# Half a first chain, loads on SyncE's queue, and softmax denominators summed on VectorE

## What is computed

```python
w_down = down_project * dg[b] + db[b];  w_up = up_project * ug[b] + ub[b]   # per batch, from cond_512
h = relu(x @ w_down) @ w_up + x                                             # low-rank adapter
paths = sigmoid(h @ Wp + bp)                                                # 8 heads, 5 levels
agree = pq * pk + (1 - pq) * (1 - pk);  sim = cumprod(agree).sum() / 5      # every query with every key
attn = softmax(where(causal, sim, -inf));  x = x + (attn @ (h @ Wv)) @ Wo
z = x @ (U[b] @ V) + bias;  U = (mu @ W_dec + b_dec)                        # batch's own weights
out = z + z @ expert_w[argmax(z @ gate_w.T)]                                # one of 8 experts
```

## Time and profile before

| | |
|---|---|
| median of 3 runs | 154.97 us |
| the profiled execution, its time | 155.55 us |
| its span, first to last instruction | 153.4 us |
| busy: TensorE, VectorE, ScalarE, GpSimd | 141.2 (92%), 83.7 (55%), 58.8 (38%), 31.2 (20%) us |
| chain that ended last: TensorE, VectorE, ScalarE | 83%, 11%, 2% |
| granted TensorE clock, mean | 0.998 |

### The profile page before, as it was taken

How to read it: one execution, slowest core, us unless ns; L and a number is a source line. 1 busy time by engine, 2 the same in 40 slices (tenths; PEclk the granted TensorE clock), 3 DMA queues, 4 the chain that set the end, 5 groups by cost and what they waited for, 6 DMA issues and landing times.

```text
span 153.4 us, 5078 instructions
## 1 busy us (share of the span) xinstructions
PE 141.2 (92%) x2296; PEld 89.8 (59%) x2296; DVE 83.7 (55%) x156; ACT 58.8 (38%) x70; POOL 31.2 (20%) x56
## 2 busy tenths in 40 slices
PE   5989678999497999999999999999999999999992
PEld 5746155554274777457656655567558577666650
DVE  0563532619966378296915483558146851985431
ACT  3013156264226342558333451573434447310010
POOL 7200004100405302640022205200222440110000
PEclk9999999999999999999999999999999999999999
DMA  4989999600011200000101000100011010110112
GB/s 121 311 320 433 448 376 353 209 4 0 0 22 17 35 0 4 0 4 0 37 3 38 34 4 0 38 0 4 34 38 38 0 38 0 38 38 34 68 38 71
DMA packets 7381, 12.50 MB, mean 81 GB/s; under 512 B 1552, under 2 KB 5808, under 8 KB 7232
## 3 DMA queue, kind: packets, MB, share of 16 engines
q10 hardware_dynamic: 2496, 7.23, 12.1%
q1 hardware_dynamic: 4768, 4.89, 9.9%
q0 software_dynamic: 96, 0.05, 1.1%
HBM read 9.95 MB, written 2.22 MB: 79 GB/s over the span
## 4 chain that ended last, share of the span: by engine, by line
PE 83%; DVE 11%; ACT 2%; issue 1%; POOL 0%; ACTq 0%; POOLq 0%; DVEq 0%
PE work L561 36%; PE c_ps L561 24%; PE s_ps L561 17%; PE work L738 3%; DVE rden L420 2%; DVE feat L552 2%; PE work L678 2%; DVE tiles L509 1%; ACT prob L365 1%; DVE h_t L455 1%; ACT phi_t L390 1%; DVE u_row L481 1%; PE work L730 1%; DVE x_t L541 1%; DVE logit L464 0%
## 5 line engine op out<-in xcount | busy, mean ns | idle before, releaser
L365 ACT ACTIVATE prob<-s_ps 128x1536 f32<-128x1536 f32 (+1 forms) x24 | 38.2, 1593 | 39.3 <-PE s_ps L561 36.3
L420 DVE RECIPROCAL rden<-c_ps 128x256 f32<-128x256 f32 x16 | 28.1, 1757 | 26.5 <-PE c_ps L561 26.5
L342 POOL TENSOR_SCALAR_AFFINE_SELECT prob<-prob 128x1024 f32<-128x1024 f32 x16 | 20.1, 1257 | 93.1 <-ACT prob L365 93.1
L561 PE MATMUL s_ps<-phi_t 32*128 32x256 f32 (+1 forms) x384 | 24.2, 365 | 1.6 <-ACT phi_t L390 1.0
L561 PE MATMUL c_ps<-prob,v_sb 128*32 128x256 f32 (+1 forms) x384 | 24.9, 346 | 0.0
L561 PEld LDWEIGHTS s_ps<-phi_t 32*128 32x128 f32 x384 | 17.4, 184 | 10.6 <-issue 6.8
L561 PE MATMUL work<-ctx_t,mix_sb 128*32 128x256 f32 x256 | 17.0, 381 | 0.4
L561 PE MATMUL work<-zo_t,gexp 128*32 128x256 f32 x256 | 16.9, 379 | 0.0
L561 PEld LDWEIGHTS c_ps<-prob,v_sb 128*32 128x32 f32 x384 | 11.5, 109 | 9.0 <-issue 2.0
L561 PE MATMUL c_ps<-prob,ones 128*32 128x256 f32 (+1 forms) x256 | 16.3, 326 | 0.0
L561 PE MATMUL work<-w_vl,h_t 128*32 128x296 f32 x208 | 14.8, 416 | 1.1 <-DVE h_t L455 0.6
(11 more groups left out here) (95 smaller groups left out, 133.4 us busy)
## 6 DMA issues: line engine op xcount, KB each, us to landing
wdec<-in_W_dec ACTq DMA_DIRECT2D x1, 3855.0 KB, 15.2
x_t<-in_x_tr SPq DMA_DIRECT2D x4, 512.0 KB, 9.3
ex_t<-in_expert_tr ACTq DMA_DIRECT2D x1, 2048.0 KB, 22.1
...
```

What stands on the lines that cost most here:

```text
L342: nc.gpsimd.affine_select(out=tri, in_=tri, compare_op=ALU.is_ge, fill=0.0, base=0, pattern=[[0, HG], [0, 2], [1, P]], channel_multiplier= ...
L365: nc.scalar.activation(prob[:, p % 2, :, 0:width(p)], s_ps[:, :, 0:width(p)], ACT.Exp).then_inc(exped, 1)
L420: link(nc.vector.reciprocal(rden[:], c_ps[m % 2][:, CW:2 * CW]))
L561: return nc.tensor.matmul(o, w, r, start=start, stop=stop, skip_group_check=True)
```

## The change

- The first chain (bias, tanh, features, `phi`) of batch 0 is done in two halves, token tiles 0 and 1 ahead of `scores(0)`, tiles 2 and 3 after it. `gup` of batches 2 and 3 moves out of the prologue into batch 0's pairs, and `gdn` of batches 1 to 3 comes ahead of `up`. There is one warm-up matmul less. The `gdn` operations on VectorE for three batches become one each.
- W_dec, mix and experts are issued by SyncE right behind x of batch 1, and not by ScalarE after `down`.
- For seven of eight long chunks (not the last) VectorE adds all four key tiles into `tiles`: the first pair's two with one instruction as before, and the second pair's with two more (1024 and 512 elements) after the mask. TensorE multiplies only the sum with `ones`, in a new step `den` that stands one pair later, ahead of `context(p + 1)`; VectorE normalises after `den`.
- The scaled copy of `phi` for the second head group goes to VectorE.
- The steps in the gaps are placed anew: `zT` one pair later, `zs` and `zo` one pair later, `zoT` behind the context and not ahead of it, `out` and `WoU` later. The `work` banks start with the other one.

The core of the diff (the rest passes the halves through the existing steps as slices):

```diff
-WARM = 9
+WARM = 8
...
+def adding(p):
+    return pair(p)[1][1] == 1 and p < ALL - 1
...
+def closes(p):
+    return pair(p)[1][1] == 1 and pair(p)[1][5] and p < ALL - 1
...
-PROLOGUE = [("gdn", (0,)), ("gup", 0), ("down", 0), ("gup", 1), ("up", 0, 0), ("up", 0, 1), ("gdn", (1, 2, 3)),
-            ("VL", 0, 0), ("VL", 0, 1), ("VL", 0, 2), ("VL", 0, 3), ("bias", 0), ("tanh", 0), ("feat", 0),
-            ("gup", 2), ("gup", 3), ("phi", 0, 0), ("phi", 0, 1), ("scores", 0), ("down", 1)]
...
+def scaler(s):
+    return "scalar" if s[2] == 0 and s[3] != SECOND else "vector"
...
+PROLOGUE = [("gdn", (0,)), ("gup", 0), ("down", 0), ("gdn", (1, 2, 3)), ("up", 0, 0), ("up", 0, 1), ("gup", 1),
+            ("VL", 0, 0), ("VL", 0, 1), *features(0, FIRST), ("VL", 0, 2), ("VL", 0, 3), ("bias", 0, SECOND),
+            ("phi", 0, 0, FIRST), ("phi", 0, 1, FIRST), ("tanh", 0, SECOND), ("scores", 0), ("feat", 0, SECOND),
+            ("down", 1)]
...
         gaps[0] += [("up", n1, 0), ("up", n1, 1)]
-        gaps[4] += [("phi", n1, 0), ("phi", n1, 1)]
+        gaps[4] += [("phi", n1, 0, ALL_T), ("phi", n1, 1, ALL_T)]
     if b == 0:
-        gaps[1] += [("VL", n1, 2), ("VL", n1, 3)]
-        gaps[2] += [("U", 1)]
+        gaps[0] = [("phi", b, 0, SECOND), ("phi", b, 1, SECOND)] + gaps[0]
+        gaps[1] += [("U", 1)]
+        gaps[2] += [("VL", n1, 2), ("VL", n1, 3)]
         gaps[3] += [("U", 3)]
-        gaps[5] += [("G", 1), ("Uadd",)]
+        gaps[5] += [("gup", 3), ("Uadd",)]
     elif n1 < B:
-        gaps[1] += [("zs", prv, ALL_T), ("zo", prv, 0), ("zo", prv, 1), ("VL", n1, 0), ("VL", n1, 1)]
-        gaps[2] += [("VL", n1, 2), ("VL", n1, 3)]
+        gaps[0] += [("WoU",)] if b == 1 else []
+        gaps[1] += [("VL", n1, 0), ("VL", n1, 1)]
+        gaps[2] += [("zs", prv, ALL_T), ("zo", prv, 0), ("zo", prv, 1), ("VL", n1, 2), ("VL", n1, 3)]
     else:
-        gaps[1] += [("zs", prv, ALL_T), ("zo", prv, 0), ("zo", prv, 1)]
+        gaps[2] += [("zs", prv, ALL_T), ("zo", prv, 0), ("zo", prv, 1)]
         gaps[4] += [("zs", b, FIRST), ("zo", b, 0)]
-    if prv >= 0:
-        gaps[3] += [("zoT", prv, 0), ("zoT", prv, 1)]
+    if prv >= 0 and n1 < B:
+        gaps[5] += [("out", prv, 1)]
...
-        gaps[0] += [("VL", n1, 0), ("VL", n1, 1)]
-        gaps[1] += [("bias", n1), ("tanh", n1), ("U", 0), ("feat", n1)]
-        gaps[2] += [("U", 2)]
-        gaps[3] += [("Q",)]
+        gaps[0] += [("U", 0)]
+        gaps[1] += [("VL", n1, 0), ("VL", n1, 1)]
+        gaps[2] += features(n1, ALL_T) + [("U", 2)]
+        gaps[3] += [("Q",), ("gup", n2)]
         gaps[4] += [("G", 0), ("ubT",)]
-        gaps[5] += [("down", n2), ("WoU",)]
+        gaps[5] += [("G", 1), ("down", n2)]
     else:
-        gaps[0] += [("zT", prv, ALL_T)]
-        gaps[3] += [("out", prv, 0)]
-        gaps[4] += [("out", prv, 1)]
+        gaps[1] += [("zT", prv, ALL_T)]
+        gaps[3] += [("zoT", prv, 0), ("zoT", prv, 1)]
+        gaps[4] += [("out", prv, 0)]
         gaps[5] += [("out", prv, 2)]
     if b >= 1 and n1 < B:
-        gaps[2] += [("bias", n1), ("tanh", n1), ("feat", n1)]
+        gaps[2] += features(n1, ALL_T)
     if prv >= 1:
-        gaps[1] += [("out", prv - 1, 3)]
+        gaps[0] += [("out", prv - 1, 3)]
...
+        ORDER += _a
+        if _p and closes(_p - 1):
+            ORDER += [("den", _p - 1)]
+        ORDER += [("context", _p)]
         ORDER += _c
-        if _p + 1 < ALL and opening(_p + 1):
+        if _p + 1 < ALL and adding(_p + 1):
...
+            sp.dma_start(x_t[:, 1], x_tr[1].rearrange("(c p) t -> p c t", p=P)).then_inc(ld_x[1], 16)
+            sp.dma_start(wdec[:], W_dec).then_inc(ld_wdec, 16)
+            sp.dma_start(mix_sb[:], mix).then_inc(ld_mix, 16)
+            sp.dma_start(ex_t[:], expert_tr.rearrange("e (c p) f -> p e c f", p=P)).then_inc(ld_ex, 16)
+            for b in range(2, B):
...
-                    if s[1] == 0:
-                        act.dma_start(wdec[:], W_dec).then_inc(ld_wdec, 16)
-                        act.dma_start(mix_sb[:], mix).then_inc(ld_mix, 16)
-                        act.dma_start(ex_t[:], expert_tr.rearrange("e (c p) f -> p e c f", p=P)).then_inc(ld_ex, 16)
...
+                elif kind == "phi" and scaler(s) == "vector":
+                    _, b, g, ts = s
+                    tok = slice(P * ts[0], P * (ts[-1] + 1))
+                    full(dve, s)
+                    nc.vector.tensor_scalar(phi_t[:, b % 2, g, tok], bank(s)[:, tok], rootc[:], None, op0=ALU.mult
+                                            ).then_inc(empty(s), 1)
...
+                elif kind == "den":
+                    dve.wait_ge(closed, closings(s[1]))
+                    normalise(chunk(s[1]))
...
+                    acc = tiles[:, chunk(p) % 2]
+                    if pair(p)[1][4]:
+                        dve.wait_ge(exped, p + 1)
+                        nc.vector.tensor_tensor(acc, both[:, :, 0, :], both[:, :, 1, :], ALU.add).then_inc(added, 1)
+                    else:
+                        dve.wait_ge(masked, masks(p))
+                        dve.wait_ge(added, adds(p) - 2)
+                        nc.vector.tensor_tensor(acc, acc, both[:, :, 0, :], ALU.add).then_inc(added, 1)
+                        dve.wait_ge(added, adds(p) - 1)
+                        nc.vector.tensor_tensor(acc[:, :, P:CW], acc[:, :, P:CW], both[:, :, 1, 0:P], ALU.add
+                                                ).then_inc(added, 1)
...
+            def denominators(p):
+                m = chunk(p)
+                pe.wait_ge(added, adds(p))
+                for h in range(HG):
+                    ins = mm(c_ps[m % 2][DH * h:DH * (h + 1), CW:2 * CW], ones[:], tiles[:, m % 2, h, :],
+                             start=False, stop=(p < ALL - 1))
+                return ins
...
-                if half and last:
-                    pe.wait_ge(added, adds(p))
-                    for h in range(HG):
-                        mm(c_ps[m % 2][DH * h:DH * (h + 1), CW:2 * CW], ones[:], tiles[:, m % 2, h, :],
-                           start=False, stop=False)
+                if p == ALL - 1:
+                    denominators(p)
...
-                    if half and first:
+                    if half and p < ALL - 1:
```

106 lines of the change are left out of this document (57 added, 49 removed).

## The result

The changed kernel takes 163.03 us, the median of four executions (160.63 to 272.1), where the kernel before takes 155.09. The ratio is 1.042, with a 95% interval of 1.026 to 1.057: slower by 4%, where I had forecast 154.4 and a range that ended at 157.4. Measured again it takes 160.28 (157.91 to 161.98, six executions), a ratio of 1.019 [1.014, 1.023]. The ratios leave out slow executions (those over 1.5% above the fastest of their kernel), which here are those whose clock fell most, so they come out nearer to 1 than the ratio of the medians, 1.051 and 1.028. The two measurements differ because TensorE's granted clock differs from execution to execution. This has to be told, since the times can't be read without it.

A forecast was written before the change was run, and what follows sets the result against it. From batch 1 on TensorE was taken as the bound, before that the chain of small steps. Terms -3.15 + 0.1 + 1.0 + 1.5 = -0.55 gave 155.0 for the profiled execution, 154.4 for the median; range 151.0 to 157.4.

The forecast's parts named there:

- step 1: Opening: one warm-up product less and a halved first chain bring the first context from 25.75 to 22.6, -3.15 us.
- step 2: Second pairs of seven long chunks: ones-products on the probabilities go, saving 4.55 us of TensorE time, counted within the batches.
- step 3: Batch 0: removed denominators -1.3, `gup` 2 and 3 +1.8, new waits of 2.75 for old ones of 3.16; net +0.1 us.
- step 4: Batches 1 and 2: late selection chain delays the V/L product; with small waits, less denominators, +0.5 us each, +1.0 together.
- step 5: Batch 3: late selections on GpSimd hold up `zoT` and the last scores by 2.15; less 0.65 of denominators, +1.5 us.
- the rival of the turns: Batch 3: VectorE's adds and GpSimd's selections take turns, costing 4.0; sum +1.3, median 155.7; chance 0.19.
- The hidden waits: Batches 1 to 3: the late selection chain's waits are mostly hidden; half of them gives -3.6, 151.3 us; chance 0.35.
- the 2 that I had set as the point: Sign: if waits on `pick` and `zo` together are under 2 us, the forecast is wrong and the kernel faster.
- VectorE's queue becomes the bound: Batches 1 and 2: VectorE's line of work delays exponents, each batch costing 1.9 instead of 0.5; 157 us; chance 0.17.
- The loads: Start: the early large load on SyncE's queue delays small loads such as bp or x; about 157.5 us; chance 0.08.

The follow-up runs named there:

- before_warm8: The kernel before with 8 warm-up products in place of 9 and nothing else; 155.70 us, ratio 1.000.
- the early chain: The changed kernel with `zT`, `zs` and `zo` moved ahead again, and in batch 3 one `out` with them; 154.07 us, ratio 0.986.
- den_tensor: The changed kernel with the long chunks' denominators back on TensorE as in the kernel before, its late selection chain kept; 156.50 us, ratio 1.005.
- late_first_add: The changed kernel with VectorE's add of the third pair in batches 1 to 3 put behind the chain from `z_nat` to `pick`; 158.84 us, ratio 1.023.
- early_batch_3: The changed kernel with the selection chain (`zT`, `zs`, `zo` of batch 2) moved ahead in batch 3 alone; 157.23 us, ratio 1.005.
- gup2_later_filled: The changed kernel with `gup` 2 one pair later and identity products in front of both waits for `zo` in batch 3; 158.82 us, ratio 1.020.
- filled_zo_wait: The changed kernel with three 128 x 128 identity products in front of each of batch 3's two waits for `zo`; 160.10 us, ratio 1.021.

## Why the prediction was wrong, point by point

**The opening (step 1) held, a little short.** First scores at 17.12 (forecast 17.15), first context at 22.96 (22.6). The gain is 2.8, not 3.15. The 0.46 for the warm-up product, taken alone in the kernel before (before_warm8), can't be told from nothing: 1.000 [0.997, 1.003].

**The removed denominators (step 2) held as a count**, seven groups fewer. What they are worth was never 4.55 by itself: taken alone with the early chain it is 1.6 to 2.1 at full clock.

**Batch 0 (step 3).** The waits at `gup` 2, `gup` 3 and `WoU` are 1.57, 0.20 and 0.77, together 2.54, against 2.75. I had them in the sum as time only.

**Batches 1 and 2 (step 4) held in the main term.** V/L begins 4.16 after the third scores (forecast 4.1), and the two waits for `pick` are 3.4 against 0.5 before, 2.9 where I had 2.8. The small ones are 0.4 more than counted: `phi_t` 0.9 and `prob` 0.2 twice, against 0.9 in all, and 0.34 for `x_t` was not in the list.

How far the first three batches were right can be read at the context of pair 17, with the same work behind it in both but for one `den`. Before, on TensorE:

```profile
111.43 0.64 PE L561 MATMUL c_ps<-tiles,ones 128*32 128x256 f32 x8
111.89 0.61 PE L561 MATMUL c_ps<-prob,v_sb 128*32 128x256 f32 x8
...
113.19 1.05 PE L561 MATMUL work<-ctx_t,mix_sb 128*32 128x256 f32 x16
```

It ended at 113.19, and in the changed kernel at 111.81. The `den` that is still due there is 0.46 (111.43 to 111.89), so the lead is 0.9, where steps 1 to 4 gave 2.05. The missing 1.1 are the small amounts named above: 0.36 in the opening, 0.4, 0.34, and 0.1 at `pick`, less 0.2 in batch 0. They all went against me.

**Batch 3 (step 5) is the term that was mis-sized most at full clock.** I put the waits for `zo` at 2.15 ("the row nearest to a queue of four GpSimd instructions is the piece of 2.34") and the rival of the turns at 4.0. The turns came: 4.67 for the four selections, 3.32 of waiting, nearer to 4.0 than to 2.15, and 0.63 for `x_t` in the tail that I had not looked at. From the lead of 0.9 to a lag of 2.4 is 3.3, which is 3.32 + 0.63 - 0.65. The choice was wrong by its own evidence. The piece of 2.34 had no add of VectorE next to it; the pair of rows with one did show that they exclude each other. The rule of the Trainium skill (SBUF — State Buffer, section SBUF: two separate sides), that the shared port pair is held for a whole instruction, gave the turns, and the trace agrees: 4.67 with three adds in the way, 2.34 without (den_tensor), 5.70 with another add moved into it (late_first_add).

So the sum at full clock, -0.55, should have been +2.35. For the median, which I took 0.58 lower, that is 157.3, just inside my range up to 157.4; the fastest of ten executions, 157.91, lies 0.5 outside it.

**What no step had is the clock, and it is the larger part of the miss in the first measurement.** The kernel before was at 0.998, and I took it as given: a term put at nothing without a reason. Each of the waits that I wrote down in steps 3, 4 and 5 can cost more than its length, since TensorE may be at 1.2 GHz for 3.4 or 6.8 us behind it. Measured, by single executions and so only roughly: 1.05 for one stretch (157.91 to 158.95), 2.2 for one in early_batch_3 (155.5 to 157.7), 0.5 for one in gup2_later_filled (158.5 to 159.0), 4 to 5 for three. The 2.2 holds a late start as well: in filled_zo_wait, counted from the first scores, a stretch at `gup` 2 is 1.5 (140.2 against 138.7). In the median the clock is 2.4 in one measurement and 5.1 in the other, where the miss at full clock is 2.9.

**The rivals.** The turns (0.19) were right in their mechanism. Their median of 155.7 does not follow from their own sum: +1.3 on 154.97 is 156.3, and 156.9 for an execution like the profiled one. Against 157.9 that is 1.1 too low, for the small amounts and the tail. The hidden waits (0.35) are out: `pick` and `zo` together are 6.7, far from the 2 that I had set as the point. That VectorE's queue becomes the bound (0.17) is the nearest in time, 157 to 159, but not in what it says: TensorE waited for no `added` and no `closed` and 0.9 in all for exponents, and VectorE's busy 101.2 is what I had counted. Its price came out by the clock, which it doesn't name. The loads (0.08) are out.
